# Graph layer with attention, linear mix and routed experts: the experts' scatters get a bound on their row numbers and lose the wait for the scatter before

## The reference, cut to what matters

```python
rh = relu(features @ router_w1 + router_b1)
expert_logits = softmax(rh @ router_w2 + router_b2)
top_w, top_i = top_k(expert_logits, 2)
routing_weights = softmax(top_w)
h1 = relu(features @ expert_w1[e] + expert_b1[e])     # for each expert e
h2 = relu(h1 @ expert_w2[e] + expert_b2[e])
expert_out = h2 @ expert_w3[e] + expert_b3[e]
x = x + sum over the two chosen experts of routing_weights * expert_out
```

## Time and profile before

| | us |
|---|---|
| median of three runs | 3224.36 |
| the profiled execution's own time | 3225.35 |
| its span in the profile | 3223.5 |
| mean granted TensorE clock over the span | 0.827 of 2.4 GHz |
| experts, first list: end of the weighted sum of tile 0 to that of tile 53 | 190.8 |
| experts, second list: the same for tiles 54 to 107 | 181.9 |

### The profile page before, as it was taken

The page is one execution under the profiler, slowest core; times in us unless marked ns, Lnnn a source line. Parts: engine busy times, 40 slices in busy tenths (PEclk is TensorE's granted clock), DMA queues, the critical chain, the costliest instruction groups (busy, mean ns, idle before and its releaser), DMA issues. The chain is left out here.

```text
span 3223.5 us, 76668 instructions
## 1 busy us (share of the span) xinstructions
PE 2658.5 (82%) x15653; PEld 2315.1 (72%) x15654; DVE 2145.0 (67%) x5435; ACT 1174.6 (36%) x4700; POOL 1899.9 (59%) x1991
## 2 busy tenths in 40 slices
PE   6689999899999999996888878888877756688897
PEld 4578788787787877865777777777777635677786
DVE  6476676666666666664777777777777655555565
ACT  3243443444344334452333333333333542222222
POOL 2466666666666666416777777777777224055564
PEclk9777777777777777797999989999998858599999
DMA  8655555555555555325666666666666247344433
GB/s 263 186 151 142 138 153 136 140 153 134 143 148 138 146 144 139 98 80 152 176 172 175 175 174 176 174 176 174 173 175 175 66 145 256 96 141 150 130 116 92
DMA packets 521893, 489.16 MB, mean 152 GB/s; under 512 B 295959, under 2 KB 431277, under 8 KB 521828
## 3 DMA queue, kind: packets, MB, share of 16 engines
q0 software_dynamic: 96384, 285.57, 31.9%
q1 hardware_dynamic: 354324, 149.37, 18.1%
q10 hardware_dynamic: 71120, 53.52, 5.3%
HBM read 406.96 MB, written 81.21 MB: 151 GB/s over the span
## 5 line engine op out<-in xcount | busy, mean ns | idle before, releaser
L666 POOL DMA_INDIRECT e_rows<-table,e_idx x1664 | 1576.3, 947 | 728.5 <-issue 405.5
L1029 PE MATMUL e_ps_sum<-e_hot,e_msg 128*128 128x129 f32 x6656 | 1190.0, 321 | 233.2 <-DVE e_msg L705 162.3
L1029 PEld LDWEIGHTS e_ps_sum<-e_hot,e_msg 128*128 128x128 f32 x6656 | 994.5, 220 | 374.2 <-ACT parts L902 224.0
L901 ACT ACTIVATE acc<-e_ps_sum 128x256 f32 x1664 | 639.2, 384 | 1384.2 <-PE e_ps_sum L1029 1191.2
L705 DVE TENSOR_TENSOR e_msg<-e_rows,e_ps_pr 128x256 f32<-128x256 f32 x1664 | 660.2, 416 | 111.0 <-PE e_ps_pr L1022 46.0
L1012 PEld LDWEIGHTS e_ps_al<-e_win,e_hotT 128*128 128x128 f32 x3328 | 481.3, 223 | 7.5 <-DVE e_hotT L696 7.5
L1012 PE MATMUL e_ps_al<-e_win,e_hotT 128*128 128x8 f32 x3328 | 473.8, 270 | 6.8 <-DVE e_hotT L696 6.8
L686 DVE TENSOR_TENSOR e_hot<-e_ps_pr,rel 128x512 f32<-128x512 f32 x416 | 286.5, 689 | 225.9 <-PE e_ps_sum L1029 192.2
L696 DVE TENSOR_TENSOR e_hotT<-e_relb,e_ps_pr 128x512 f32<-128x512 bf16 x416 | 281.8, 677 | 1.4 <-PE e_ps_al L1012 1.0
L902 ACT ACTIVATE parts<-e_ps_sum 128x4 f32 (+1 forms) x1664 | 279.6, 168 | 0.0
L1918 ACT ACTIVATE x_h<-x,eb 128x128 f32<-128x128 f32 x216 | 67.4, 363 | 274.8 <-PE x L1987 274.8
(11 more groups left out here) (294 smaller groups left out, 3221.0 us busy)
## 6 DMA issues: line engine op xcount, KB each, us to landing
e_relb<-rel_rows SPq DMA_DIRECT2D x104, 512.0 KB, 5.1
e_win<-table SPq DMA_DIRECT2D x1664, 4.0 KB
e_rows<-table,e_idx POOLq DMA_INDIRECT x1664
e_eattr<-in_edge_b SPq DMA_DIRECT2D x104, 128.0 KB
e_xT<-turned_x ACTq DMA_DIRECT2D x100, 128.0 KB
e_xr<-in_x ACTq DMA_DIRECT2D x100, 128.0 KB
node<-acc SPq DMA_DIRECT2D x25, 512.0 KB, 3.8
table<-t_row ACTq DMA_DIRECT2D x25, 272.0 KB, 4.2
```

The source lines that it names most:

```text
L666: nc.gpsimd.indirect_dma_start(out=rows[q][:, k, :], out_offset=None, in_=table, in_offset=bass.IndirectOffsetOnAxis(ap=idx[:, q, k:k + 1] ...
L901: nc.scalar.activation(acc[:, :, bass.ds(at[k], P)], ps_sum[(k + q) % 3][:, :, 0:P], ACT.Copy).then_inc(s["window"], 1)
L1029: op = nc.tensor.matmul(ps_sum[(k + q) % 3][:, a, 0:WIN], msg[:, k % RM, a * P:a * P + P], hot[:, q, k, :], start=(a == 0), stop=True, ski ...
```

## The change

The wait for the preceding store is gone, and both scatters get a bound: an index over N - 1 = 6249 is skipped, without an error.

```diff
@@ experts, store(t)
                 u = t % RY
                 if t == 0:
                     pool.wait_ge(s["pad"], 16 * 4)
-                else:
-
-                    pool.wait_ge(s[f"put{(t - 1) % RY}"], 16 * ((t - 1) // RY + 1))
                 if t < TH:
                     nc.gpsimd.indirect_dma_start(
                         out=mid, out_offset=bass.IndirectOffsetOnAxis(ap=who[:, t:t + 1], axis=0),
-                        in_=y[:, u, :], in_offset=None).then_inc(s[f"put{u}"], 16)
+                        in_=y[:, u, :], in_offset=None, bounds_check=N - 1, oob_is_err=False).then_inc(s[f"put{u}"], 16)
                 else:
                     nc.gpsimd.indirect_dma_start(
                         out=out, out_offset=bass.IndirectOffsetOnAxis(ap=who[:, t:t + 1], axis=0),
-                        in_=y[:, u, 0:F], in_offset=None).then_inc(s[f"put{u}"], 16)
+                        in_=y[:, u, 0:F], in_offset=None, bounds_check=N - 1, oob_is_err=False).then_inc(s[f"put{u}"], 16)
```

## The result

The changed kernel takes 3215.47 us (median of 14 executions, 3206.01 to 3220.94) against 3223.41 us of the kernel before (14 executions beside them, 3213.28 to 3231.04). The ratio is 0.9972, 95% interval 0.9960 to 0.9983: faster by 0.17 to 0.40%, 5 to 13 us, where 20 were predicted. The sign was right and the size was not: the time lies at the upper edge of the range, just outside it.

The account below looks back on a forecast made before the run. The prediction took POOL's waits for store landings to bound the first list. Gains of 14.2 + 1.8 + 3.0 + 1.3 = 20.3 us took the profiled 3225.35 to 3205.0, a median of 3204 us, range 3198 to 3215.

Parts of the forecast that it names:

- the chain of stores: First list: each store waits for the preceding one's landing, which paces everything at 3.59 us a tile.
- A clean cycle of twelve tiles: Both lists: two turns' five steps plus two boundaries take 40.31 us, against 43.09 and 40.98 before.
- a late tile: Second list, tiles 72 to 77: 15.98 us instead of 15.31 was read as delay from a late tile.
- last sign of being wrong: Twelve tiles still at 41 us or more, without slow L1875, PE waiting on landings over 4.2 us, or clock under 1.00.
- Term 1: First list, tile 0 to 53: from 190.8 to 176.6 us, gain 14.2 us.
- Term 2: Between the lists: tile 53's store begins earlier and the fetch of the sums moves with it, gain 1.8 us.
- Term 3: Second list: 0.67 us less per twelve tiles over 54 tiles, gain 3.0 us.
- Term 4: End of the kernel: the last store can begin at 3210.81 instead of 3212.09, gain 1.3 us.
- Term 5: Bound on the scatters: POOL's cost taken as 0, within -0.1 to +0.97 us; nothing taken for shorter last landings.
- Nearly every store starts 0.18 us ahead of a copy: Stores beside DVE's weight copy (L1928): store stays at 0.99 us and copy at 0.69, so nothing was added.
- that rival: Clock in the first list: grant falls to 0.75 as PE fills, +80 us and more, about 3290; chance 0.02.
- The case that came nearest: Experts' lists: stores and fetches hinder each other, or a bound costs 0.6 to 0.8 us; middle 3212, chance 0.17.

Follow-up runs that it names:

- before_early: Kernel before, waits kept and no bound, with ScalarE's register load moved from the loop boundary into its idle time: 3223.8 us, ratio 0.9986 to the kernel before.
- aligned_before: Kernel before with the list of experts at 8 entries (32 bytes) per turn instead of 6: 3935.4 us on another chip, ratio 0.9977 to the kernel before.
- changed_again: The changed kernel itself, nothing altered, run again on a third chip as base for others: 3215.1 us, ratio 0.9964 to the kernel before.
- no_wait_no_bound: Changed kernel without the bound; empty places get rows of their own, second list goes to a scratch tensor: 3215.5 us, ratio 0.9962 to the kernel before.
- copy_without_lock: Changed kernel with VectorE's weight copy done as a maximum over an axis of size 1: 3212.9 us, ratio 0.9951 to the kernel before.
- aligned_again: Changed kernel with the list of experts at 8 entries (32 bytes) per turn instead of 6, third chip: 3202.0 us, ratio 0.9917 to the kernel before.
- aligned_early: Changed kernel with 8 list entries per turn and ScalarE's register load moved into its idle time: 3197.6 us, ratio 0.9911 to the kernel before.
- bound_only: Kernel before with the bound of 6249 added to both scatters, every wait for the preceding store kept: 3236.8 us against 3227.05.
- bound_no_skip: Kernel before, waits kept, with a bound of 6399 on the scatters that skips nothing: 3949.7 us, one execution on another chip.

## Why the prediction was wrong, point by point

1. *What bounds the first list: the chain of stores.* Right, and shown three ways. With the wait gone POOL's waits for landings are gone; before_early and aligned_before, which keep the wait, stay at 42.9 and 42.3 us.
2. *"A clean cycle of twelve tiles is then 2 x 15.31 + 4.21 + 5.48 = 40.31 us."* This is the step that failed. It took the fast turn for the rule and the slow one, 15.98, for a fast one with a late tile, so it put the register loads' part of the slow turn at nothing. The slow turn is slow by itself: ScalarE's register load for the turn that follows takes 1.33 to 1.78 us instead of 0.75, on the path. Free of the stores a cycle takes 41.2 to 41.3 us, 0.9 more than said, nine cycles: 8.1 us. 20.3 - 8.1 is 12.2, against 10.3 in the profile. The late tile was no error of reading: in the kernel before the slow turn of tiles 72 to 77 has both delays, ready within 0.04 us of each other (view of the load's line, and timeline):

```profile
L1904 ACTq TENSOR_LOAD <-owner x1: 1337/1337/1337, 3102.3 to 3102.3; - x1
```

```profile
3103.87 0.38 ACT L1911 ACTIVATE x_yT<-x_y 128x256 f32<-128x256 f32 x1 [1.41 <-issue]
...
3103.91 0.44 PE L1981 MATMUL x_y<-ident,x_y 128*128 128x128 f32 x2 [0.24 <-DMA x_y<-mid,who]
```

Taking one away leaves the other. The rows were at hand: the prediction's argument from the clean pieces, "with the same work", compared only turns of the short kind, and both register loads stood in the chain of waits. Its own last sign of being wrong, "a twelve-tile cycle still at 41 us and more without any such row", is what came.
3. *Term 1, first list, 14.2 us.* 8.4 in the profile, 8.6 in changed_again.
4. *Term 2, between the lists, 1.8 us.* 2.0, from other parts: the store of tile 53 starts 1.3 us less late (0.81 instead of 2.11 behind its sum), and its landing is 0.64 us shorter (2.88 for 3.52), since all its rows are skipped. The prediction had taken nothing for that, so the near agreement is luck.
5. *Term 3, second list, 3.0 us.* -0.7 and +0.7 in two profiles, so nothing. Here the loads set nearly the whole pace already.
6. *Term 4, the end, 1.3 us.* 1.1 (13.45 us from tile 107's sum to the span's end before, 12.36 after).
7. *Term 5, the bound costs POOL nothing.* Wrong, with next to no effect on the pace: the start is 0.53 us later behind a sum, and the instruction 0.02 longer. It lay within the bounds given (-0.1 to +0.97). With the collision of point 8 it used the slack up: in the steady turns POOL has 1.35 for the store, 0.30, 0.97 for the fetch and 0.46 up to the next store, 3.08 in all, and that 0.46 is what the wait for the sum leaves, since these stores too start 0.81 us behind it. The smallest idle time seen there is 0.35. Each end of a list bears the 0.53 in full. A first guess of mine after the result, theory S, made it the cause, and three runs refused it.
8. *"Nearly every store starts 0.18 us ahead of a copy."* It starts 0.22 us inside one and takes 1.35 us. On this the Trainium skill, SBUF — State Buffer, section "Who interferes with whom", was the better guide: the second to start is blocked until the first is through. The copy here ended 0.46 us after the store's start, and the store was 0.34 longer. In the other order it does not hold as it stands: stores 0.31 us ahead of a copy took 1.11 us in no_wait_no_bound, where by the rule the copy should have waited, and the copy kept its 0.68. Only a copy that starts late in POOL's instruction is longer: 0.75 us at 2942.38 in the kernel before, 0.76 us behind the start of a fetch.
9. *The fetch's wait for the store of two tiles before* never ended last, as said; PE waited 1.4 us for fetches in the first list, the first tile left out. The clock stayed at 1.00 over 2822 to 3004 us, the whole first list, so that rival is out too. (Its price, "+80 us and more", was low: 3.08 us at 0.75 is 1.03 us more, 111 us for 108 steps.)
10. The chances: faster by over 0.2% had 0.84, which came true by a little (0.28%). The case that came nearest was the one whose middle was 3212, by another mechanism than it named.

What stays open: ScalarE's long load took 1.35 us in the kernel before (at 3143.34 us) and 1.50 to 1.78 in the changed one, and five steps of the slow turn in the second list 16.0 and 16.1 to 16.2. The bound isn't the cause (no_wait_no_bound has 16.1 to 16.2), nor the collision with the copy (copy_without_lock has the same). Nor was it tried why single turns early in the first list take up to 16.8 us in the aligned kernels as well, and the first of the second list 16.6 to 17.5; behind the gap the clock was below 1.00 for some 20 us.

## What to carry to other kernels

A stretch that runs well is a measure for the rest only if all parts of the period are in it: lay out the steps of two or three whole turns and explain every one that differs before calling the best one clean. Take a wait's name from the chain, which knows the sequencers' register loads, not from the idle time before an instruction. When a wait is removed, price what stood second on every engine of the loop; here it kept 8 of the 20 us, and another layout of one small list removed it, with 13 us gained in the time and 15 in the experts' stage.

## What the runs showed of the hardware

- A register load from SBUF takes 0.75 us (ScalarE, six registers), 0.60 to 0.85 (VectorE, eight) and 0.82 (TensorE, six) in aligned_again, where it starts on a multiple of 32 bytes from the start of its list; TensorE's first takes 1.17. At a stride of 24 bytes every second one is long, up to 1.78 (ScalarE) and 1.91 (TensorE) in the changed kernel and 2.28 (VectorE) in the kernel before; the others, at multiples of 48, are short. That the boundary is 16 bytes is inferred from the alternation; no other stride was tried. The address isn't all: ScalarE's loads at good addresses took up to 1.14 us in aligned_early, where they stand inside the turn, and 0.94 to 1.07 in no_wait_no_bound. The Trainium skill, DMA: Bandwidth & Descriptors, section "Latency and other measured facts", gives a floor of about 600 ns for such a load, which VectorE's aligned loads meet, and says nothing of the address.
- With a bound an indirect scatter starts 0.81 instead of 0.28 us behind the sum that releases it, and 0.86 instead of 0.80 behind a landing (medians of bound_only and the kernel before). Where POOL waited for nothing, one store started 0.35 us behind a fetch with the bound (2836.17 in the changed kernel) and one 0.31 without (2863.59 in no_wait_no_bound). The instruction itself takes 1.01 instead of 0.99 us. Whether rows are skipped makes no difference to the start.
- A scatter of 128 rows of 2112 bytes lands 0.67 us sooner if all of them are skipped (POOL's wait for it: 1.87 us in bound_only and the changed kernel, 2.54 in bound_no_skip and the kernel before).
- The weight copy and POOL's indirect DMAs lengthen each other by their order: a store that starts 0.22 us inside the copy takes 1.35 us instead of 1.01 (1.01 beside an operation of VectorE that is a maximum), one 0.31 us ahead of it 1.11 instead of 0.99.
